# Second batch's gathers issued in waiting pairs, and its moments taken up eight units later, in a four-stage transformer kernel

## The reference

```python
x = _layernorm(x + _L0_attn_ref(x, ...))   # linear attention, 16 heads
x = _layernorm(x + _L0_ffn_ref(x, ...))    # 8 experts, top 2, capacity 1.2, gather and scatter by token
x = _layernorm(x + _L1_attn_ref(x, ...))   # causal softmax attention, 16 heads of 8, ALiBi
x = _layernorm(x + _L1_ffn_ref(x, ...))    # 32 experts, top 4, and a shared gated layer
```

## Time and profile before

| | us |
|---|---|
| three runs | 1370.04, 1372.16, 1377.62 (median 1372.16) |
| the profiled execution | 1373.69 |
| its span | 1372.0 |
| PE busy | 1068.4 (78%) |
| DVE busy | 813.6 (59%) |
| ACT busy | 546.6 (40%) |
| POOL busy | 472.3 (34%) |

### The profile page before, as it was taken

The page is one execution under the profiler, slowest core; times in us unless marked ns, Lnnn a source line. Parts: engine busy times, 40 slices in busy tenths (PEclk is TensorE's granted clock), DMA queues, the critical chain, the costliest instruction groups (busy, mean ns, idle before and its releaser), DMA issues. The chain is left out here.

```text
span 1372.0 us, 20820 instructions
## 1 busy us (share of the span) xinstructions
PE 1068.4 (78%) x7039; PEld 635.7 (46%) x7039; DVE 813.6 (59%) x2128; ACT 546.6 (40%) x876; POOL 472.3 (34%) x468
## 2 busy tenths in 40 slices
PE   5762139913899999999999998987889979878851
PEld 4661128711244344534444443442378768744521
DVE  4766730142867877777877787788247424454532
ACT  1330014403056466646466653554543324321221
POOL 3110035355315210530025410334343514555654
PEclk9975559965589999979999998999999989998975
DMA  4214004322213211220123233251146666521121
GB/s 109 91 52 127 1 19 116 114 45 78 69 44 89 55 38 43 65 66 18 52 51 104 60 73 87 68 186 53 38 131 183 170 187 174 141 76 38 37 72 50
DMA packets 111908, 112.19 MB, mean 82 GB/s; under 512 B 17445, under 2 KB 95013, under 8 KB 108773
## 3 DMA queue, kind: packets, MB, share of 16 engines
q1 hardware_dynamic: 72614, 71.35, 18.3%
q0 software_dynamic: 12048, 25.71, 6.8%
q10 hardware_dynamic: 27144, 13.83, 3.5%
HBM read 65.22 MB, written 41.94 MB: 78 GB/s over the span
## 5 line engine op out<-in xcount | busy, mean ns | idle before, releaser
L2144 DVE TENSOR_REDUCE maxima<-psum 128x1 f32<-128x512 f32 (+4 forms) x624 | 390.9, 644 | 128.6 <-PE psum L1963 70.2
L2081 ACT ACTIVATE probs<-psum 128x1024 f32<-128x1024 f32 (+3 forms) x384 | 300.6, 809 | 296.7 <-PE psum L1978 215.6
L1958 PE MATMUL psum<-ka,qa 75*128 75x512 bf16 (+3 forms) x528 | 167.0, 349 | 27.3 <-DVE maxima L2144 14.0
L114 POOL DMA_INDIRECT f_got<-expert_out,dense x128 | 128.0, 1000 | 129.4 <-DMA f_got<-expert_out,dense 60.1
L1991 PE MATMUL psum<-probs,v_wide 128*32 128x512 f32 (+3 forms) x1536 | 171.1, 519 | 0.0
L1974 PE MATMUL psum<-qa,ka 78*128 78x512 bf16 (+3 forms) x528 | 147.4, 343 | 5.4 <-ACT probs L2081 4.7
L1451 POOL DMA_INDIRECT sorted<-x_rows,to_row x76 | 75.2, 990 | 218.1 <-ACT probs L2081 116.8
L2482 ACT ACTIVATE g_silu<-psum 128x512 f32<-128x512 f32 x80 | 47.8, 597 | 204.0 <-PE psum L2417 87.6
L1377 POOL DMA_INDIRECT w_gu<-expert_out,to_row x64 | 64.5, 1008 | 145.9 <-ACT probs L2081 104.7
L2393 PE MATMUL psum<-w_gu,g_xT 128*128 x384 | 100.7, 408 | 11.7 <-DVE g_h L2554 6.6
L1958 PEld LDWEIGHTS psum<-ka,qa 75*128 75x128 bf16 x528 | 46.9, 99 | 131.9 <-DVE maxima L2144 96.6
(11 more groups left out here) (327 smaller groups left out, 1715.7 us busy)
## 6 DMA issues: line engine op xcount, KB each, us to landing
g_rows<-sorted SPq DMA_DIRECT2D x192, 64.0 KB
expert_out<-g_y ACTq DMA_DIRECT2D x48, 256.0 KB
qa<-q_steps SPq DMA_DIRECT2D x30, 192.0 KB
ka<-k_steps SPq DMA_DIRECT2D x10, 576.0 KB
w<-in_W SPq DMA_DIRECT2D x16, 256.0 KB
w_gu<-in_gu SPq DMA_DIRECT2D x4, 1024.0 KB
sorted<-blank SPq DMA_DIRECT2D x54, 64.0 KB
q_steps<-w_gu SPq DMA_DIRECT2D x12, 256.0 KB
```

Of the source, the lines that this page charges most:

```text
L114: self.pool.indirect_dma_start(oob_is_err=False, **transfer).then_inc(self.landed[u], 16)
L1958: mm = pe.matmul(bank[:, h * width:(h + 1) * width], qa[b][0:ROWS_MAX, h0 + h, qt * P:(qt + 1) * P], ka[b][0:ROWS_MAX, h0 + h, seg * HALF: ...
L2081: act.activation(probs[k % PRING][:, 2 * pair:2 * pair + 2, 0:w], PS[:, 2 * pair:2 * pair + 2, 0:w], ACT.Exp).then_inc(exps, 1)
L2144: dve.tensor_reduce(maxima[:, seg, h0:h0 + heads, qt], bank[:, 0:heads * width].rearrange("p (h k) -> p h k", h=heads), AX.X, ALU.max).the ...
```

## The change

`gather` gets a second wait, which applies to the second batch only (b = 1) and to its tiles 1 to 7: before the two gathers of tile t, POOL waits until those of tile t - 1 have landed. DVE's wait for the combined rows and the moments move from unit 26 to unit 34.

```diff
-SECOND_MOMENTS_AT = 26
+SECOND_MOMENTS_AT = 34
...
                 def gather(b, t):
                     if b and t == 0:
                         pool.wait_ge(S.scaled[0], b * TB)
+                    if b and t:
+                        pool.wait_ge(Q.got_here[(t - 1) // 2], (b * 2 + (t - 1) % 2 + 1) * K0 * 16)
                     for k in range(K0):
                         emit_gather0(pool, S, Q, b, t, k)
```

## The result

| | before | after |
|---|---|---|
| median of nine runs each, us | 1371.13 (1363.25 to 1379.93) | 1383.66 (1374.63 to 1389.07) |
| ratio, 95% interval | | 1.0088 (1.005 to 1.0125) |
| the profiled execution, its span | 1373.69, 1372.0 | 1387.08, 1385.4 |
| first gather of the second batch | 316.31 | 321.85 |
| first maxima, behind that gather | 26.3 | 25.6 |

The change makes the kernel slower by 0.88%, 12.1 us of 1371.13. The head of attention alone, from the second batch's first gather to the first scores, is 13.0 us longer in the two profiled executions. The profiled execution of after reached the head 5.5 us later than that of before did, a scatter of the stages ahead of it, so I compare places behind that first gather and not behind the start of the span. "Combination done" is read at the start of POOL's copy behind it.

A forecast was written before the change was run, and what follows sets the result against it. Attention is bound by TensorE, so the change is worth its shift of the first scores: 375.7 + 10.92 + 0.9 = 387.5 against 379.30, 8.2 us later. 1373.7 + 8.2 = 1381.9, or 1380.4 beside the median; range 1369 to 1387.

The forecast's parts named there:

- worse than the sum: Second batch's gathers: each pair behind the fourth at 10.1 us, start 12 us later still, 1392; chance 0.15 beyond 12 us.
- signs of being wrong: Late pairs under 6 us apart, no DVE wait at unit 34, or scores 8 us late without the whole.
- The 0.41: Chance of a whole time within 0.5%, 6.9 us, of no change: 0.38 and 0.03 from two rivals.
- The new waits: POOL's second-batch gather pairs: quiet interval 1.30 + 3.13 + 0.77 = 5.20 us, busy 1.30 + 5.27 + 0.6 = 7.17, against 2.64 before.
- The last landing and the combination: POOL, behind the eighth pair: combination starts 5.27 us after the last gather, at 367.2, and ends 8.47 later, at 375.6.
- From the combination to the scores: First step: scores follow the combination by 10.92 + 0.9 us; the moments' move costed at nothing, between -0.7 and +0.7.
- The start of the sum: First scores of the unchanged kernel, taken at 379.30 us, against which 387.5 was 8.2 us later.
- The four engines: DMA engines at 345 to 350 us: share 0.26 read as all six stores queueing on the same four of sixteen.
- The quiet pace throughout: Rival: stores hold up no pair of gathers, scores at 377.7, 1370.6; chance 0.38 with mixtures short of half a per cent.
- The rival without a wait for DVE: Intervals near 4.2 us, combination done by 358, `ka` landing up to 5.3 us earlier: 1366.9 at most; chance 0.04.
- The interval of 4.2: Gather pair by the skill page's landing: 1.30 + 2.15 + 0.77 = 4.2 us, not used because the trace's 3.23 disagreed.
- The clock: Half clock behind the first scores, granted at 0.50 from 380 to 390 us: moves with them, nothing within 2 us.

The follow-up runs named there:

- after_wide: The changed kernel with each of SP's stores of the parts cut in four, one for each step's 32 rows; ratio to before 1.0107 (1.0035 to 1.018).
- moments_only: The kernel before with only the moments moved from unit 26 to unit 34, without the new waits; ratio to before 1.0049 (1.0018 to 1.008).
- moments_again: A repeat of the kernel before with only the moments moved to unit 34; ratio to before 0.9995 (0.9964 to 1.0026).
- before_again: The kernel before once more, unchanged; ratio to before 1.0016 (0.9987 to 1.0045).
- gathers_behind_ka: The kernel before, with POOL starting none of the second batch's gathers until the first step's operands have landed; one execution, 1387.32 us.
- the first set: Runs made together: moments moved alone, waits alone, the change with moments at unit 44, the change with stores cut in four; ratios 1.0049, 1.0204, 1.0087, 1.0107.

## Why the prediction was right, and where its sizes were off

The forecast was slower by 8.2 us, 1380.4, with the scores of the first step 8.2 us late; measured are 12.1 us, 1383.66, and 13.0. The mechanism was right at each of its places: the combination late, DVE idle ahead of unit 34 and released by L1410, PE idle beside it, no gain from `ka`, and the loss handed on. The size was 4 to 5 us short, and at its border: 12.1 us stands where the forecast's own 7 to 12 us (0.40) end and "worse" (0.15) begins, and the head's 13.0 beyond it. One of its signs of being wrong came true in part, a late pair under 6 us apart (the sixth interval, 5.12). The 0.41 for a time within half a per cent of before did not come true.

*The new waits.* The sum had three quiet intervals of 5.20 and four busy ones of 7.17, 44.3 us. Measured: 5.22, 6.39 and 5.85, then 10.12, 7.67, 5.12 and 10.46, 50.8 us. The quiet value held for the first alone, before SP and ACT load the operands; leaving the second and third at it missed 1.8 us, one of which is POOL's, whose fourth gather took 2.02 us instead of 1.00. The busy value was a mean of two gathers of later batches; the true ones lie 2.1 us below it to 3.3 above, 4.7 us too little in the sum. The rival "worse than the sum" took 10.1 us from the last gather of before and I set it aside as a backlog that pairs can't have. Two of the four were that long all the same: what they wait behind is not the gathers' own backlog but, as after_wide shows for the first of them, the stores'.

*The last landing and the combination.* 3.3 us in place of 5.27, since the loads were over by then, which by luck took back 2.0 of the 6.5 us that the intervals were short; the combination took 8.41 for 8.47. With the intervals, 63.9 for 59.3.

*From the combination to the scores.* 12.1 us for the 11.8 of the sum. The moments moved at no cost to the head, as moments_only and moments_again show.

*The start of the sum.* The scores were taken as 63.0 us behind the first gather, from one execution in which `ka` landed latest of the four with these stores and gathers; the others have 59.4, 59.6 and 60.6. The late combination does not move with `ka` (63.1 to 63.9 in three kernels), so beside the 60.6 of before_again the same sum, whose scores stand 71.2 us behind the gather, would have said 10.6 us and not 8.2. That the whole time shows 12.1 beside this pair's 13.0 is within its interval, 7 to 17 us.

*The four engines.* The inference from a share of 0.26 was right in what it led to: after_wide removes the two long intervals in the middle by spreading the stores. The Trainium skill (DMA: Bandwidth & Descriptors, on why a DMA increments its semaphore by 16) has a transfer split over the largest number of engines up to 16 that divides the slowest dimension of both its sides. By the share of 0.65 where that dimension is 32, against 0.26 where it is 4, the runs agree.

*The rivals.* The quiet pace throughout is what after_wide nearly has, up to its last pair, and with that pair it is still 4.5 us behind before. The rival without a wait for DVE falls twice: no interval is under 5.1 us, and `ka` landed no earlier with fewer gathers beside it (gathers_behind_ka, and the four kernels that wait), so nothing was seen to win on that side. The 2.15 us of the Trainium skill (DMA: Bandwidth & Descriptors, on the anatomy of a DMA by the gpsimd path), counted from the gather's start, gave 4.2 us an interval. The shortest seen is 5.1: the second gather of a pair needs 3.3 us at the least from its start to POOL's next instruction, 1.00 of it for making its descriptors and 2.30 behind that. Counted from the end of the 1.00, the figure is near what the runs show with little else in flight: as an estimate by that page, 1.30 + 1.00 + 2.15 + 0.77 = 5.2 us, and the first interval was 5.22. The interval of 4.2 had left the 1.00 out.

*The clock.* Costed at nothing within 2 us; the half-clock stretch behind the first scores is 11.4 us, and was 11.7.

## What to carry to other kernels

A wait for a landing in a queue costs its landing and the start of the next transfer, 5.1 to 10.5 us a pair here against 2.6 without it, by what else is in flight at that moment; count it once for each wait, at that moment's load, and compare the sum with the slack of whoever consumes the last one. Take the start of such a sum from more than one execution: here it moved by 3.6 us between four. Before thinning transfers to free the path of another, take them away altogether in one run: if the other lands no earlier, they were not in its way. And look at the DMA share while a large transfer runs: where it is low and others wait, the transfer may lie on few engines, and can be held behind what is urgent.

## What the runs showed of the hardware

Six stores of 256 KB, whose slowest dimension is 4, kept the DMA engines' share at 0.26 and 102 GB/s with no gather and no operand load left in flight (345 to 350 us of the kernel before). The same bytes in stores of 32 rows, with other transfers beside them, ran at a share of 0.65 and 166 to 186 GB/s and let the loads behind them start 8 us sooner. Two gathers of 64 KB, alone in their queue, needed between 3.3 and 9.3 us from the start of the second to that of POOL's next instruction, by what else was in flight. What remains open: why the first set's whole times lie some half a per cent above their heads, whether the loads are what makes the last interval long, and why `ka` lands anywhere from 22.6 to 26.3 us in kernels that differ in nothing ahead of it.
